# Two-layer transformer kernel: routing of the last chunk, order of the second layer's experts, and smaller edits beside them

## The reference, cut to what matters

```python
# layer 1, attention: k and v normalised over each head's 8 channels
kv  = einsum('bhqd,bhqe->bhde', k, v) / Q * temperature + attn_bias
att = einsum('bhqd,bhde->bhqe', q, kv) + x
x   = x + ga * (gelu(att @ p1_w.T + p1_b) @ p2_w.T + p2_b + x_normed)
# layer 1, experts
scores = softmax(xf @ w_router)
expert_weights, top_experts = top_k(scores, 2)
# slot = expert * 1024 + number of earlier pairs of this expert; dropped from 1024 on
h = gelu(einsum('ech,ehf->ecf', xb, w1))        # ff = 512
y = einsum('ecf,efh->ech', h, w2)
out[token] += weight * y[slot]                  # then + bias
```

## Time and profile before

| | us |
|---|---|
| median of 3 runs (1098.78 to 1101.27) | 1099.19 |
| the profiled execution's own time | 1099.11 |
| its span in the profile | 1097.4 |
| PE busy in the span | 948.9 |
| DVE / ACT / POOL busy in the span | 686.4 / 560.5 / 319.9 |

### The profile page before, as it was taken

The page is one execution under the profiler, slowest core; times in us unless marked ns, Lnnn a source line. Parts: engine busy times, 40 slices in busy tenths (PEclk is TensorE's granted clock), DMA queues, the critical chain, the costliest instruction groups (busy, mean ns, idle before and its releaser), DMA issues.

```text
span 1097.4 us, 20608 instructions
## 1 busy us (share of the span) xinstructions
PE 948.9 (86%) x7904; PEld 772.6 (70%) x7904; DVE 686.4 (63%) x2261; ACT 560.5 (51%) x940; POOL 319.9 (29%) x397
## 2 busy tenths in 40 slices
PE   3668999899999999999999999999999733599970
PEld 2435555455689888889888889988888621499960
DVE  8777887767587553755776666567776765032225
ACT  2287687867756645554554445445445311344410
POOL 6844161400100210203113130312232040486550
PEclk9698999999999999999999999999999955699995
DMA  6344433463920000000000000000000200122217
GB/s 163 101 144 148 130 121 115 131 189 83 243 78 1 1 2 1 1 1 21 1 6 16 8 13 2 20 1 15 6 16 5 76 20 2 49 64 81 76 37 235
DMA packets 85373, 66.48 MB, mean 61 GB/s; under 512 B 8115, under 2 KB 75814, under 8 KB 85275
## 3 DMA queue, kind: packets, MB, share of 16 engines
q1 hardware_dynamic: 80852, 56.87, 17.8%
q0 software_dynamic: 4352, 8.28, 2.3%
q10 hardware_dynamic: 70, 0.02, 0.0%
HBM read 33.82 MB, written 31.59 MB: 60 GB/s over the span
## 4 chain that ended last, share of the span: by engine, by line
PE 67%; DVE 16%; ACT 7%; issue 4%; DMA 3%; SPq 2%; POOL 1%; POOLq 0%; DVEq 0%; ACTq 0%
PE psum L1364 22%; PE psum L1341 17%; PE psum L1196 3%; DVE maxes L1687 2%; PE psum L1134 2%; PE psum L1104 2%; PE psum L1416 1%; PE psum L1255 1%; PE psum L1275 1%; PE psum L1150 1%; PE psum L1177 1%; PE psum L1297 1%; PE psum L1126 1%; DMA routed<-empty_row 1%; SPq L993 1%
## 5 line engine op out<-in xcount | busy, mean ns | idle before, releaser
L1364 PEld LDWEIGHTS psum<-ew,big 128*128 128x128 f32 x2560 | 316.1, 192 | 19.5 <-ACT big L2236 3.2
L1364 PE MATMUL psum<-ew,big 128*128 128x128 f32 x2560 | 322.4, 276 | 1.1 <-ACT big L2236 1.0
L2236 ACT ACTIVATE big<-psum,cols 128x512 f32<-128x512 f32 x256 | 174.2, 687 | 186.2 <-PE psum L1341 185.1
L1341 PE MATMUL psum<-parts,q_stack 128*128 128x512 f32 x640 | 226.0, 434 | 0.6 <-DVE parts L2008 0.5
L1687 DVE TENSOR_REDUCE maxes<-psum 128x4 f32<-128x1024 f32 (+1 forms) x96 | 113.5, 1217 | 21.8 <-PE psum L1150 21.5
L1341 PE MATMUL psum<-parts,k_stack 128*128 128x512 f32 x320 | 126.8, 396 | 0.0
L1341 PEld LDWEIGHTS psum<-parts,q_stack 128*128 128x128 f32 x640 | 107.4, 193 | 11.4 <-DVE parts L2008 0.9
L2502 POOL DMA_INDIRECT routed<-big,slot_i x64 | 63.1, 986 | 147.6 <-DVE big L2002 129.8
L1807 DVE SCALAR_TENSOR_TENSOR hT<-psum,gates,hT 128x128 f32<-128x128 f32 x256 | 71.9, 343 | 31.1 <-PE psum L1364 30.9
L2512 POOL DMA_INDIRECT answers<-hT,to x64 | 62.3, 974 | 35.8 <-issue 19.0
L1341 PEld LDWEIGHTS psum<-parts,k_stack 128*128 128x128 f32 x320 | 60.8, 190 | 13.8
(11 more groups left out here) (359 smaller groups left out, 1717.4 us busy)
## 6 DMA issues: line engine op xcount, KB each, us to landing
q_stack<-q_pieces SPq DMA_DIRECT2D x32, 192.0 KB
k_stack<-k_pieces SPq DMA_DIRECT2D x32, 192.0 KB
routed<-empty_row SPq DMA_DIRECT2D x4, 1040.0 KB, 11.3
big<-routed SPq DMA_DIRECT2D x16, 260.0 KB, 2.8
answers<-gb_tok SPq DMA_DIRECT2D x4, 1024.0 KB, 10.2
q_pieces<-gb_tok SPq DMA_DIRECT2D x16, 192.0 KB, 2.1
k_pieces<-gb_tok SPq DMA_DIRECT2D x16, 192.0 KB, 2.2
x<-in_L_attn_x SPq DMA_DIRECT2D x4, 512.0 KB, 6.1
```

Source lines behind the costliest of these rows:

```text
L1341: last = eng.matmul(bank(i), w1_part(wp, e)[:, fs], parts[2 * xk + xp][:, :], start=n == 0, stop=n == 2)
L1364: last = eng.matmul(psum[:, i, k * C:(k + 1) * C], hid[:, r, f, k * P:(k + 1) * P], ew2[:, e, f, :], start=f == 0, stop=f == FC - 1)
L2236: eng.activation(hid[:, held("hid", "up", n, e, f), f, :], bank(held("bank", "up", n, e, f)), ACT.Relu, bias=col("L0_ffn_b1", e * FC + f)) ...
```

## The change

- A list `ORDER` of units: first half 0 (slots 0 to 511) of all 8 experts, then half 1. The first 8 units (`EARLY`) wait for `rt_d` of the first 14 sequences only, not for the last chunk's two.
- The last chunk (g = 7) gives its pairs slots from each expert's last slot downwards (`upside`). It has 512 tokens, and a token goes to an expert at most once, so it never reaches slots 0 to 511. Whether a pair is dropped is decided by its count as before.
- `w2` is loaded in two halves: experts 0 to 3 after `down` of expert 3 of the last chunk, 4 to 7 after that of expert 7.
- All steps of the front parts of chunks 6 and 7 get `urgent += 8` (they stand in the queues of DVE, ACT and POOL as if ready 8 us earlier); on PE their rank is ahead of all expert work, as before.
- The slot numbers are counted on PE: `first_slots`, the pairs so far (`chosen`) and the counts in the chunk are accumulated in one PSUM bank by 6 small matmuls per chunk (7 in the last) instead of 2; the DVE part of `rt_c` is gone, `rt_w` has 7 operations (9 in the last chunk) instead of 16, `rt_k` 12 instead of 15 and takes in `rt_p`. The softmax's division is a step of its own, `rt_v`, not ahead of the top 2. `rt_b` is on ACT alone.
- `rsqrt` has 8 operations instead of 10, everywhere.
- `la_r` handles a chunk's two sequences together; the multiplication is a step `la_m`; `la_s` no longer waits for `la_q`. The last 4 sequences scale and shift on DVE (`la_h`) instead of POOL.
- `ag` is on DVE alone; `sg_r` moves from DVE to ACT; `bias` from POOL to DVE.

```diff
+ORDER = [(e, half) for half in range(CAP // CHUNK) for e in range(NE)]
+EARLY = NE
+LAST = 4
...
+        if chain is not None and self.hurried is not None and self.hurried <= chain[0] <= self.hurried + 1:
+            urgent += 8.0
...
-    p.step("w2", work="sp:.1 dma:12", after=[(("down", NCH - 1, NE - 1, CT - 1), "pe")])
+    for h in range(2):
+        p.step("w2", h, work="sp:.1 dma:7", after=[(("down", NCH - 1, 4 * h + 3, CT - 1), "pe")])
...
+        p.step("la_r", n, work="dve:3.2", after=[("la_s", b) for b in batches], rank=rank, chain=(20 + n, BPC * n, 2),
+               squares=[tiles[b][2] for b in batches])
...
+            if b < B - LAST:
+                scaled = p.step("la_g", b, work="pool:2.7", after=[("la_m", b), ("gam",)], ...)
+            else:
+                scaled = p.step("la_h", b, work="dve:1.35", after=[("la_m", b), ("gam",)], ...)
...
+    p.hurried = 20 + NCH - 2
     for n in range(NCH):
...
-        e, at = u * CHUNK // CAP, 9 * MOE + 100 * u
-        p.step("fetch", u, ..., after=[("rt_d", b) for b in range(B)] + ...)
+        e, at = ORDER[u][0], 9 * MOE + 100 * u
+        here = B - BPC if u < EARLY else B
+        p.step("fetch", u, ..., after=[("rt_d", b) for b in range(here)] + ...)
...
-    spread(1, [*[("ag", b) for b in range(B)], ("up2", 1, 0)])
+    spread(1, [*[("ag", b) for b in range(B)], *[("la_q", b) for b in range(B - BPC, B)]])
...
             def fetch(u):
                 k = u % RINGS
+                e, half = ORDER[u]
                 for r in range(2):
-                    w.wait_ge(routed_out[r], 16 * TPB * TOPK * B // 2)
+                    w.wait_ge(routed_out[r], 16 * TPB * TOPK * ((B - BPC if u < EARLY else B) // 2))
...
-                eng.dma_start(xb[:, k, :, :], routed_v[u]).then_inc(xb_in[k], 16)
+                eng.dma_start(xb[:, k, :, :], routed_v[CAP // CHUNK * e + half]).then_inc(xb_in[k], 16)
...
             def rt_c(g):
...
+                eng.matmul(slots(0), before[:, :], sel[:, :, :], start=True, stop=False, skip_group_check=True)
+                eng.matmul(slots(0), ones_b[:, :], all_of(first_slots), start=False, stop=False, skip_group_check=True)
+                eng.matmul(slots(0), ones_b[:, :], all_of(chosen), start=False, stop=False, skip_group_check=True)
+                for t in range(1, RG):
+                    last = eng.matmul(slots(t), ones_b[:, :], sel[:, 0:RG - t, :], start=False, stop=t == RG - 1,
+                                      skip_group_check=True)
+                if g == NCH - 1:
+                    last = eng.matmul(psum[:, i, RG * NE:(RG + 1) * NE], ones_b[:, :], chosen[:, :], start=True, stop=True)
...
+            def rt_w(g):
...
+                eng.tensor_tensor(slots_f, slots, wide(limits), ALU.is_ge)...
+                if g < NCH - 1:
+                    eng.scalar_tensor_tensor(slots_f, slots_f, float(SLOTS), slots, ALU.mult, ALU.add)...
+                else:
+                    eng.tensor_tensor(upside[:, :], upside[:, :], psum[..., RG * NE:(RG + 1) * NE], ALU.add)...
+                    eng.scalar_tensor_tensor(slots_f, slots_f, float(SLOTS), slots, ALU.mult, ALU.subtract)...
+                    eng.tensor_tensor(slots_f, slots_f, wide(upside), ALU.add)...
...
+            def ag(b):
+                eng.tensor_tensor(y[:, ts, :], y[:, ts, :], gb_tok[:, b, :]..., ALU.mult)...
+                eng.tensor_tensor(x[:, ts, :], x[:, ts, :], y[:, ts, :], ALU.add).then_inc(sem("ag"), 1)
...
+            def la_r(n):
+                for h in range(BPC):
+                    eng.tensor_reduce(vv[:, h * TPB * G2:(h + 1) * TPB * G2], squares[h]..., X_AXIS, ALU.add)...
+                eng.scalar_tensor_tensor(vv, vv, 1.0 / HD, least[:, :]..., ALU.mult, ALU.add)...
+                rsqrt(vr, vv, squares[0][:, 0:BPC * TPB * G2]).then_inc(sem("la_r"), 1)
...
+                eng.copy(rows_buf[:, r, :, :, C], dest[:, :, TPB * b:TPB * (b + 1)]...)
+                eng.copy(rows_buf[:, r, :, :, 0:C], psum[..., 0:S]... .to_broadcast([P, TPB, TOPK, C])).then_inc(sem("rt_b"), 1)
```

More of the change, by code:

```diff
@@ L580, in route @@
-        p.step("rt_w", g, work="dve:3.3", after=[("rt_c", g)], rank=rank, chain=chain)
-        for b in range(g * RG // TPB, (g + 1) * RG // TPB):
-            bank = p.buffer("bank")
-            p.step("rt_b", b, work="pe:.22 act:.27 dve:.5", after=[("ln_t", 1, 1, b), ("rt_w", g)]
-                   + ([("rt_d", b - 2)] if b >= 2 else []), rank=rank, chain=chain, opens=[(0, bank)], closes=[(2, bank)], bank=bank)
-            p.step("rt_d", b, work="pool:5 dma:3.5", after=[("rt_b", b), *fills], rank=rank, chain=chain)
+        one("rt_s", g, "pe:.81 dve:.45", [("ln_t", 1, 1, b) for b in batches], rank, chain)
@@ new lines, in route @@
+        p.step("rt_e", g, work="act:.25", after=[("rt_s", g)], rank=rank, chain=chain)
+        p.step("rt_k", g, work="dve:2.5", after=[("rt_e", g), ("tab",)] + ([("rt_w", g - 1)] if g else []), rank=rank, chain=chain)
+        slots = p.buffer("bank")
+        p.step("rt_c", g, work="pe:.4", after=[("rt_k", g)], rank=rank, chain=chain, opens=[(0, slots)], slots=slots)
+        p.step("rt_v", g, work="dve:.8", after=[("rt_k", g)] + [("rt_d", b - 2) for b in batches if b >= 2], rank=rank, chain=chain)
@@ L587, in order_steps @@
+        p.step("rt_w", g, work="dve:1.3", after=[("rt_c", g)], rank=rank, chain=chain, urgent=1, closes=[(0, slots)], slots=slots)
+        for b in batches:
+            one("rt_b", b, "pe:.22 act:.8", [("ln_t", 1, 1, b), ("tab",)] + ([("rt_d", b - 2)] if b >= 2 else []), rank, chain)
+            p.step("rt_d", b, work="pool:5 dma:3.5", after=[("rt_b", b), ("rt_v", g), ("rt_w", g), *fills], rank=rank, chain=chain)
+    p.hurried = 20 + NCH - 2
     for n in range(NCH):
         for b in range(BPC * n, BPC * n + BPC):
-            tile = p.buffer("tmp")
@@ L590, in order_steps @@
-            p.step("ag", b, work="pool:.7 dve:.35", after=[("mix", n, NE - 1), ("am_x", n)] + [("sg_m", 0, k) for k in range(B // 4)],
-                   chain=(20 + n, b, 0), opens=[(0, tile)], closes=[(1, tile)], tmp=tile, rank=MOE - 300 + b)
+            p.step("ag", b, work="dve:.75", after=[("mix", n, NE - 1), ("am_x", n)] + [("sg_m", 0, k) for k in range(B // 4)],
+                   chain=(20 + n, b, 0), rank=MOE - 300 + b)
         statistics(1, 0, n, [("ag", b) for b in range(BPC * n, BPC * n + BPC)], (20 + n, 0, 1), MOE - 300)
-        for b in range(BPC * n, BPC * n + BPC):
-            linear_attention(b, MOE - 300 + b, (20 + n, b, 2))
+        linear_attention(n, MOE - 300)
@@ L757, in build @@
         magic = sb("magic", [P, 1])
+        least = sb("least", [P, 1])
         wo = sb("wo", [P, C])
@@ L2023, in ans, with bias @@
                 last.then_inc(sem("ans"), 1)
+            def bias(b):
+                k, xs = held("tmp", "bias", b), x[:, TPB * b:TPB * (b + 1), :]
+                w.wait_ge(*done("sg_m", 1, b // 4))
+                for c in cleared("tmp", "bias", b):
+                    w.wait_ge(*c)
+                eng.tensor_tensor(T(k)[:, 0:C], gb_tok[:, b, :], row("L1_ffn_bias"),
+                                  ALU.mult).then_inc(chain.sem, chain.more())
+                w.wait_ge(chain.sem, chain.n)
+                eng.tensor_tensor(xs, xs, T(k)[:, 0:C].unsqueeze(1).to_broadcast([P, TPB, C]),
+                                  ALU.add).then_inc(sem("bias"), 1)
             def sum_(n):
```

395 lines of the change are left out of this document (192 added, 203 removed).

## The result

The changed kernel takes 1032.41 us (median of 4 runs, 1028.6 to 1033.65) against 1098.99 us (1098.57 to 1101.27) for the kernel before in the same group: ratio 0.9384 [0.9355, 0.9414]. The profiled execution took 1028.6 us, the fastest of the four, with a span of 1026.9. The forecast was 1046, with a range of 1034 to 1062.

A forecast was written before the change was run, and what follows sets the result against it. Latency bounds the kernel: PE mostly idles some 80 us before the second layer's experts. Experts start at 877, plus 117, 10 and 5 ends PE at 1009 against 1062.1, 53 earlier; other edits 0: 1099.1 − 53 = 1046, range 1034 to 1062.

The forecast's parts named there:

- The hole: Between the last chunk's mixture and the second layer's experts, some 80 us: early units start at 877 instead of 945.1.
- Chunk 7 in time: Last chunk's rows fetched by 942.5, PE needing them at 950: 8 us to spare, so PE bounds.
- Rivals A: Chunk 6's chain stays at 70.3 us, so PE starts experts at 896.5: 1065 in all; chance 0.13.
- B: Chunk 7 sets the end, its chain not shortened because experts share DVE, ACT and POOL: 1054; chance 0.10.
- C: Slower: chunk 7's PE steps each fall behind a block of down2, 75 us more chain: 1112; chance 0.03.
- E: More than forecast: no PE stall and start at 874, 1038, or 1035 with earlier stages' gains; chance 0.06.
- The other edits: Ahead of 865 PE is bound by its own work; small matmuls, DVE relief, rsqrt, bias: net 0, bounds −2 and +5.
- PE's block: PE from first expert rows at 877 to its end at 1009: 117 experts, 10 chunk 7's work, 5 stalls.
- Stalls: PE waiting on ACT's table changes beside the experts: up to 7 loads instead of 3, 1.28 us each; 5 us taken.
- the 117: PE's 16 expert units at 6.78 us each, with sg_m and a start at the lower clock: 117.0, as before.
- The tail: Behind PE's end: last answers, last sends, reading back and sums, 35.3 us plus 1.7 around the span, unchanged.
- Rival D: Each of 4 added ACT table changes stops ACT another 1.4 us and PE waits: 1051.5; chance 0.08.

The follow-up runs named there:

- Experiments 1: Changed kernel with only the early start taken away, all 16 units waiting for the routing of all 16 sequences: 1075.75 us, ratio 0.9775.
- 2: Kernel before with only the early start added (unit order, early units, halved w2, last chunk's slots downwards): 1070.01 us, ratio 0.9714.
- control: The changed kernel run again, unaltered, beside the 5-operation rsqrt variants: 1036.24 us, ratio 0.941 to the kernel before.
- (3): Changed kernel with the old rsqrt of 10 operations instead of 8 in both layers, orders the same: 1044.41 us, ratio 0.9495.
- experiment 11: Changed kernel with the linear attention's Gelu (la_1) also in its tanh form: 1031.95 us, ratio 0.9409.
- experiments 5: Changed kernel without the urgency of 8 us for the front parts of chunks 6 and 7: 1039.64 us, ratio 0.9463.
- 8: Changed kernel with sg_m no longer waiting for chunk 7's la_q, to fill PE's hole: 1036.11 us, ratio 0.9431.
- (15): Changed kernel with the 5-operation rsqrt in the first layer only, 8 in the second: 1032.3 us, ratio 0.9363.

## Where the prediction was right, and which of its terms failed

- **The hole.** Forecast: first expert transpose 877, 5.3 us behind the last `mix`. Measured 868.75, 6.1 behind its row's end. Right, and only moved by what came before. Chunk 6's chain from its last `mix` to its first write was to take 50.2 us and took 48.5 (803.45 to 851.91); first write 9.4 us ahead of the last `mix`, measured 10.7. Experiments 1 and 2 bear out that it takes both the early units and the shorter chains. I had the first `fetch`, delayed by the second half of `w2`, decide the start. It is one of two that decide it: DVE's `ln_z` of chunk 7 ends PE's 6.8 us of idling, and the `fetch` lands 0.4 us later, with a wait of 0.2 us for PE's weight load, and of 0.7 for PE in the control.
- **Chunk 7 in time.** Forecast 54.3 us from the last `mix` to its first write, with 9 for queueing; measured 50.0 (862.6 to 912.6). PE reached unit 8 without a wait, so PE bounds, as said, but the margin is smaller than the forecast's 8 us: unit 8's `fetch`, issued at 923.9, lands at 926.7, and PE starts on it at 929.65. Rivals A, B and C are out. Nearest came E (more than forecast, 1035), to which I had given 0.06; the time is 2.6 us beyond it.
- **The first step that failed: "The other edits", put at net 0 with bounds −2 and +5.** The time to the last `mix` fell by 9.1 us, in the control by 4.1. I had the shorter `rsqrt` at under 1 us there. Taken alone it is worth 9.4 us in the kernel before and 9 to 12 in the changed one, and in the changed one only 1.7 of those lie behind the last `mix` (3): 3 `rsqrt` per chunk of the second layer, 2 operations of 0.2 to 0.3 us less in each, are 1.4 us of chain per chunk, 11 over eight, and 6.6 of them showed up in the mixture. The mistake was the sentence that PE is bound by its own work before 865. The 93% busy of the earlier trace rows hold for 25 us only. Over the kernel before's whole mixture PE is busy 573.7 of 584.3 us, 98%, and yet the chain beside it is felt: 10.0 of the 10.6 idle us are waits for DVE and ACT, and the 4 us stretches at 647 and 651, around the wait of 1.9 us in the earlier trace rows, have a mean clock of 0.87 and 0.70, 1.7 us lost; the changed kernel has no such stretch in the mixture. I had priced PE's added matmuls and the first layer's statistics, and read the earlier trace rows as the sum of a few stalls rather than as the sign that the chain is felt. By the same cut, the changed kernel with the old `rsqrt` has its last `mix` at 876.0 against 871.4 before: the other early edits together gain nothing and may lose some us, which the scatter leaves open. Which of them would lose it wasn't tried.
- **The second step that failed: PE's block, 132 forecast, 125.3 measured** (868.75 to 994.02; control 125.6). Two terms were too large. Stalls: 5, against 1.5 measured at ACT (5 table loads, not 7). And the 117 carried the cold start of before: its clock was 0.96 over 115 us, some 4.6 us lost, against 0.99 over 126 in the changed kernel, 1.3 lost, since PE comes out of a hole of 7 us and not of 74. Chunk 7's own work at full clock, 10 forecast, is what remains: 125.3 − 1.5 − 1.3 less 117 − 4.6 is 10.1. The cold start was in the row that I read; when a hole closes, its warm-up goes too. With the control's numbers this is the largest miss, 6.4 us.
- **The tail: 2.4 us shorter,** forecast unchanged. It isn't in my terms. The last two `ans` are 5.9 us apart in the changed kernel and 1.8 in the kernel before, and the last `send` is issued 6.0 us behind the end of the last `down2` (1000.02) instead of 9.1 (1071.20). The two `ans` before:

```profile
1060.36 1.12 DVE L2021 TENSOR_SCALAR hT<-psum,big 128x128 f32<-128x128 f32 x4 [9.31 <-PE psum L1364]
...
1062.15 1.13 DVE L2021 TENSOR_SCALAR hT<-psum,big 128x128 f32<-128x128 f32 x4 [0.59 <-PE psum L1364]
```

- **Rival D** (tables) is out for the changed kernel: PE's waits for ACT sum to 1.5 us, and experiment 11 gains nothing. What it describes is seen in experiments 5 and 8. The Trainium skill (ScalarE: Activation LUTs, "What ACT_TABLE_LOAD costs") adds a drain of 1.38 us to a load of 1.28. ACT's timeline of the changed kernel has the load and no drain, the activation follows at once:

```profile
904.72 1.28 ACT L2355 ACT_TABLE_LOAD   x1
906.01 0.23 ACT L2355 ACTIVATE scores<-scores 128x32 f32<-128x32 f32 x1
906.26 1.28 ACT L2300 ACT_TABLE_LOAD   x1
907.55 0.60 ACT L2300 ACTIVATE big<-psum 128x512 f32<-128x512 f32 x1
```

Added up in the profiled execution: start of the experts 8.3 us earlier than forecast (9.1 from before the last `mix`, less 0.8), the block 6.7 shorter, the tail 2.4: 17.4 of the 17.5 between 1046.1 and 1028.6. The profiled execution was the fastest of four; the median is 3.8 higher. In the control (1034.3) it is 4.1 − 1.8, 6.4 and 3.0: 11.7 of 11.8. One slip of reading changes nothing: in the earlier trace rows slice 8 is at 8 tenths, not 9.

## What to carry to other kernels

- A chain of small operations beside an engine that is 98% busy isn't free because it is "beside": where the busy engine's order is fixed and it has steps of the chain in it, operations taken off the chain may show. Here the step from 10 to 8 gave 6.6 of 11 us of chain, and that from 8 to 5 at most 2 of 17 (an estimate: 3 operations of 0.2 to 0.3 us in 3 `rsqrt` per chunk); so no fixed price holds, but zero is wrong too.
- Closing a gap gives its length, and its warm-up as well; and splitting work so that the next stage starts on the part that is ready pays in full only if that part's own chain is done before the gap. Alone the early start gave 31 us and the shorter chains with the other edits 25; together they gave 12 more than the sum.
- Before filling a gap with work from elsewhere, look at what the planner then lays in the other engines' queues: here two more table loads on ACT ate the gain.

## What was not expected of the hardware

- A wait of PE of 2.0 us in the middle of dense work was followed by 4 us at a mean clock of 0.57 (8), between the levels 1.2 and 2.4 GHz and near the lower, while the wait of 1.30 us in the changed kernel's stretch from 840 to 860 us left it at 1.00. The waits of 2.3 us (8, at 911.7) and of 1.9 us (kernel before, at 647 to 649) were followed by a fall too.
- One program, in one group, ranges over 10 us (control, 1031.99 to 1042.54); even side by side, a difference of 3.9 us (15) was not told from none.
